# Two more matmuls of 127 columns in each step of the two relation passes of a four-layer graph network

## The reference, cut to what matters

```
h = einsum('ni,rio->rno', x, W)
seg = dst * num_rels + etype
sums = segment_sum(h[etype, src], seg)        # one sum per (node, relation)
cnt = segment_sum(ones, seg)
mean = sums / maximum(cnt, 1)
out = mean.reshape(N, num_rels, do).sum(1) + x @ W_root + b
```

## Time and profile before

| | us |
|---|---|
| median of 3 runs (lowest, highest) | 3812.71 (3811.78, 3816.45) |
| the profiled execution | 3823.57 |
| its span, first to last instruction | 3821.7 |
| mean granted TensorE clock over the span | 0.743 |
| first relation pass, from its first to its last addition on DVE | about 1077 to 2322 |
| dense stage between the passes | about 2322 to 2514 |
| second relation pass | about 2514 to 3759 |

### The profile page before, as it was taken

The page is one execution under the profiler, slowest core; times in us unless marked ns, Lnnn a source line. Parts: engine busy times, 40 slices in busy tenths (PEclk is TensorE's granted clock), DMA queues, the critical chain, the costliest instruction groups (busy, mean ns, idle before and its releaser), DMA issues.

```text
span 3821.7 us, 59833 instructions
## 1 busy us (share of the span) xinstructions
PE 2532.7 (66%) x21427; PEld 1819.2 (48%) x21427; DVE 2517.1 (66%) x6311; ACT 485.3 (13%) x906; POOL 1959.8 (51%) x2108
## 2 busy tenths in 40 slices
PE   3766689989746565666555558965555655656556
PEld 1222265574435444444444446754444444444446
DVE  5999954464267666666666666666666666666667
ACT  2444441151110000000000003510000000000000
POOL 1887800000256666666666662146666666666661
PEclk9999989989865666566666668966666666666667
DMA  1000000000111111111111111111111111111111
GB/s 51 1 1 1 1 6 1 1 2 1 39 52 44 45 44 45 44 45 44 45 45 45 45 45 49 75 60 44 45 44 45 44 45 44 45 45 45 44 45 32
DMA packets 76098, 137.92 MB, mean 36 GB/s; under 512 B 29902, under 2 KB 44640, under 8 KB 75810
## 3 DMA queue, kind: packets, MB, share of 16 engines
q0 software_dynamic: 53120, 108.90, 10.9%
q1 hardware_dynamic: 18934, 24.46, 1.8%
q10 hardware_dynamic: 3756, 0.73, 0.2%
HBM read 116.35 MB, written 17.62 MB: 35 GB/s over the span
## 4 chain that ended last, share of the span: by engine, by line
PE 45%; DVE 28%; issue 11%; another core or an unknown queue 8%; POOL 3%; DMA 2%; ACT 2%; DVEq 1%; ACTq 1%; SPq 0%; POOLq 0%
PE banks L565 26%; DVE adj L1429 15%; DVE hi_hot L1131 6%; PE banks L497 6%; PE banks L490 3%; DVE lo_hot L1139 3%; PE banks L609 2%; POOL adj L711 2%; PE banks L621 2%; DMA adj<-table,adj 2%; PE banks L654 1%; DVEq L1427 1%; PE banks L472 1%; POOL lo_hot L685 1%
## 5 line engine op out<-in xcount | busy, mean ns | idle before, releaser
L565 PE MATMUL banks<-adj 128*128 128x129 f16 x13280 | 1486.3, 291 | 1026.5 <-DVE adj L1429 739.7
L711 POOL DMA_INDIRECT adj<-table,adj x1660 | 1573.3, 948 | 946.8 <-issue 402.1
L565 PEld LDWEIGHTS banks<-adj 128*128 128x128 f16 x13280 | 1199.5, 132 | 1317.9 <-issue 1161.6
L1429 DVE TENSOR_TENSOR adj<-adj,banks 128x516 f32 x1660 | 1143.0, 689 | 844.5 <-PE banks L565 480.7
L1413 DVE TENSOR_SCALAR adj<-adj 128x512 f16<-128x512 f16 x1660 | 697.1, 420 | 0.0
L685 POOL TENSOR_SCALAR lo_hot<-minus_iota,zT 128x128 f16<-128x128 f16 x392 | 332.4, 865 | 140.4 <-PE banks L445 77.1
L445 PE MATMUL banks<-hi_hot,lo_hot 128*128 128x400 f16 x977 | 267.0, 365 | 128.0 <-DVE hi_hot L1131 73.5
L1131 DVE TENSOR_SCALAR hi_hot<-iota,zT 128x400 f16<-128x400 f16 x977 | 266.0, 338 | 21.5 <-PE banks L445 21.4
L692 POOL MEMSET adj<- 128x1548 f16 x1 | 1.4, 1388 | 470.4 <-PE banks L497 470.4
L445 PEld LDWEIGHTS banks<-hi_hot,lo_hot 128*128 128x128 f16 x977 | 97.4, 100 | 297.9 <-issue 240.4
L497 PE MATMUL banks<-adj,split 128*128 128x512 f16 (+1 forms) x1190 | 235.7, 356 | 0.0
(11 more groups left out here) (219 smaller groups left out, 1625.6 us busy)
## 6 DMA issues: line engine op xcount, KB each, us to landing
adj<-table,adj POOLq DMA_INDIRECT x1660
table<-adj SPq DMA_DIRECT2D x25, 512.0 KB, 2.6
table<-split SPq DMA_DIRECT2D x6, 256.0 KB, 2.3
out_dram<-xres SPq DMA_DIRECT2D x6, 256.0 KB
adj<-in_L_gnn_W_dram SPq DMA_DIRECT2D x1, 1024.0 KB, 7.4
adj<-in_L_gnn_W_dram SPq DMA_DIRECT2D x2, 512.0 KB, 9.0
adj<-scr_index SPq DMA_DIRECT2D x1, 830.0 KB
scr_index<-adj SPq DMA_DIRECT2D x1, 512.0 KB
```

Source lines behind the costliest of these rows:

```text
L565: m = e.matmul(ps[:, g * CH // 2:g * CH // 2 + b - a], hot[:, s, g * P:g * P + P], gath[:, s, a:b], start=(q == 0), stop=(q == 1), skip_gr ...
L711: e.indirect_dma_start(gath[:, s, 0:2 * D], None, table, bass.IndirectOffsetOnAxis(ap=index[:, which, j:j + 1].bitcast(U32), axis=0)).then ...
L1429: e.tensor_tensor(a, a, ps[:, :].rearrange("p (g d) -> p g d", g=G)[:, :, 0:D + 1], ALU.add).then_inc(accumulated, 1)
```

## The change

In each step, for the first two of the four blocks, one more matmul follows the two that are there. It has the same stationary operand, 127 columns of the gathered rows as the moving one, and writes the 127 columns of the block's 256 that no instruction reads. The last matmul of a step, which raises `scattered`, stays what it was.

```diff
+FILL = 2
...
                         for q, (a, b) in enumerate([(D, 2 * D + 1), (0, D)]):
                             m = e.matmul(ps[:, g * CH // 2:g * CH // 2 + b - a], hot[:, s, g * P:g * P + P],
                                          gath[:, s, a:b], start=(q == 0), stop=(q == 1), skip_group_check=True)
+                        if g < FILL:
+                            e.matmul(ps[:, g * CH // 2 + D + 1:(g + 1) * CH // 2], hot[:, s, g * P:g * P + P],
+                                     gath[:, s, 0:CH // 2 - D - 1], start=True, stop=True, skip_group_check=True)
                     m.then_inc(scattered, 1)
```

## The result

The changed kernel took 3842.18 us (median of 4 runs, 3838.39 to 3848.62), beside 3814.24 us before (4 runs, 3811.78 to 3816.45): a ratio of 1.0075, 95% interval 1.0058 to 1.0093, so **28 us slower**. I had forecast 3713 us. The profiled execution took 3843.84 us with a span of 3842.0.

What follows compares the result with a forecast made beforehand. Bound: relation passes at 1.50 us a step, above POOL's 1.25 us floor, because completions are seen late. Longer waves at 1.44 save 100 us: 3823.6 - 100 = 3723.6, less 10.9 for the median gives 3713 us; range 3540 to 3885.

Steps and rivals of the forecast that it cites:

- The bound of the kernel: Relation passes: 1.50 us a step, filled by no engine; POOL's gather floor is 1.25; completions are seen late.
- If that phase is what decides, a wave carries one to three more steps: Waves in the passes: completions falling inside a POOL gather are seen in time; pace 1.44 us a step, 100 us less.
- I take 0: Waits for a single step, 320 to 446 of them: added matmuls cost between 0 and 94 us, taken as 0.
- cover: Wave's pause: PE finishes about 0.8 us later, still 1 us ahead of the release, so added matmul time is hidden.
- A faster PE clock as such buys next to nothing here: Single-step waits in the passes: 0.41 us less matmul time was read as starting DVE only 0.01 us sooner.
- the 1.36 and 1.37 us: Times read from a step's first matmul to DVE's start, with 0.61 and 1.02 us of matmuls respectively.
- the bound of 0.35 us: Single-step waits: extra completion time, 1.37 - 1.02, above which added matmuls would delay DVE.
- slower: Rival, lone-step waits and wave starts: later completions shift everything, 58 to 80 us more, 3871 to 3893; chance 0.31.
- the clock would be near 0.8: PE in the passes: ten matmuls per step lift the granted clock from 0.65 to an expected 0.8.
- Same: Rival: release hangs on POOL and DMA events alone, pauses swallow the work; 3813 us within 8; chance 0.22.
- Gather beat: Rival: high clock keeps completions in time, passes run at 1.25 to 1.35 us a step, 3398 to 3564; chance 0.12.
- signs listed: In the profile: L565 x16600, waves of six or more, POOL idle below 947 us, passes about 1195, clock near 0.8.

Runs made afterwards that it cites:

- e15: Kernel before with plain SyncE DMAs for POOL's gathers in the first pass (other rows added) and four bare weight loads per step in the second: 3397.55 us, ratio 0.8898.
- e1: Changed kernel with its two added matmuls cut from 127 columns to 8, same place and count: 21.6 us slower than the kernel before (3816.17 us).
- e2: Kernel before plus four constant-operand matmuls of 127 columns at the start of each step (first pass from step 100): 55.6 us slower than before.
- e3: Kernel before plus four constant-operand matmuls of 127 columns per step, placed behind the matmul that raises scattered: 56.0 us slower than before.
- e4: Kernel before with the high parts' four matmuls of each step left out, so the sums lack them: 66 us less than before (3816.17 us).
- e17: Kernel before plus four bare weight loads per step in both passes, slow kind: 3839.23 us beside 3813.61, ratio 1.0065.
- e18: Kernel before plus eight already satisfied PE wait instructions at the start of each first-pass step: 3806.64 us beside 3784.21, ratio 1.0056.

## Why the prediction was wrong, point by point

**The bound of the kernel** was read rightly as far as it went: no engine fills the 1.50 us, POOL could go at 1.25, and the difference is completions seen late. The fast kind confirms the floor to 0.01 us. That the lateness has to do with POOL's gathers was a guess from the timing of one wave, and e15's first pass bears it out.

**"If that phase is what decides, a wave carries one to three more steps"**: this is the step that failed, and with it the sign. The phase itself moved as forecast, and it bought nothing. Before, on the slow kind, the last matmul of 1138 steps ended (by its modelled end) inside a gather and of 322 in POOL's 0.30 us between two; an update was recorded within 0.3 us for 48% of the first and 2% of the second, so the trace seems to bear the rule out. After, 1319 ended inside and only 18 between, but of the 1319 only 14% were updated that soon; in e1, with two short matmuls, 2% of 1278. On the fast kind it makes no difference where they end: nearly all are prompt. The cost goes by the count each time, whether the added work lies ahead of the completion (e2), behind it (e3) or is a fraction as long (e1). The waves became shorter in steps. The commonest wave of several steps has 5 before, 4 after and in e1, three or four in e2 and e3, and 8 in e4. That is 32 to 48 matmuls, or 64 to 96 matmuls and loads, and it isn't the matmuls alone that end it: bare loads (e17) and satisfied waits (e18's first pass) make waves of 4 with the eight matmuls as they were, and e18's second pass, without the waits, has waves of 5. I had three completions of one wave to rest a rule on, and a rule that needs them to be right to 0.2 us.

**"I take 0" for a lone step, and all edits priced by time on PE.** I priced an added matmul by its length and found cover for all of it. The cover was real: 3320 matmuls of 0.056 us or more are over 180 us, and 28 came through. But on the slow kind each further instruction, matmul or weight load, has a price that no cover takes. The burst spacings, measured apart from the times, give 4.2 ns; with four per step that is 16.8 ns x 1660 = 28 us, the whole result in size, though the recorded bursts hold only a third of it. No row of before shows it, since every step there has the same sixteen; the lower bound of 0 had no measurement under it.

**"A faster PE clock as such buys next to nothing here"** stands, but not for the reason given. The earlier trace rows pair each step's matmuls with the addition of another step. PE may be up to three steps ahead of DVE, and the n-th addition belongs to the n-th step (1660 of each are recorded):

```profile
2599.88 1.77 PE L565 MATMUL banks<-adj 128*128 128x129 f16 x16
...
2607.08 0.69 DVE L1429 TENSOR_TENSOR adj<-adj,banks 128x516 f32 x1
```

The addition at 2605.09 is that of a step begun at 2599.88; the step begun at 2603.73 was added at 2607.08, 3.35 us later, and the one begun at 2612.69 at 2617.37, 4.68 us later. So the 1.36 and 1.37 us measure no step, and with them fall the bound of 0.35 us that "slower" was to be decided by and the argument for 0 at a lone step. In prompt completions (fast kind) the clock is worth 0.41 us a step, 1.20 against 0.79. It buys nothing because the time goes to the late completions on the one kind and to POOL's beat on the other. That the clock would be near 0.8 was right (0.777). The rule of the Trainium skill, "TensorE: Matmul & The Clock Gate", section "A second HAM failure mode: psum-queue depth-cycling", would charge the swing of the clock; with the swing all but gone (0.90 in the passes of the changed kernel on the fast kind, 0.88 overall in e2) nothing came back, so no run here bears it out for this loop.

**The rivals.** "Slower" had the sign, a price of 58 to 80 us where 28 came, and the wrong mechanism: e3 has its four matmuls behind the completion, and pays as much. "Same" is what the fast kind does, though not because pauses swallow the work: there are none. "Gather beat" describes the kernel before itself on that kind, with the low clock that I thought it couldn't have. The range, 3540 to 3885, held the time, 3842. Of the signs listed, L565's count (13280 + 3320) and the clock came as forecast, POOL's idle time rose where it should have fallen, and the wave was the first thing to say that the theory was wrong.

**Left open.** Why a job is of the one kind or the other. By what path POOL's gathers hold up PE's updates, whether it is their issue or their transfers that do it, whether DVE's work beside POOL's has a part in it, and why a wave ends where it does. Whether the 4 ns is spent fetching an instruction, issuing it or retiring it: instruction packets grow with the count in every run (180, 206, 228; 128 in e4), so they can't be told apart; the line of the burst spacings speaks for retiring, but the waits scatter about it. That each step's share stands once in the length of its wave is argued from 16.8 ns = 4 x 4.2, not shown. No version here that fetches the right rows beats both kernels; the plain DMAs would, by 14% on the fast kind, but not with rows picked by an index, and a gather that covers two steps at once wasn't tried.

## What to carry to other kernels

Where a loop is bound by the round trip of small completions, count its instructions, not only their time: on the slow kind each PE instruction, even a wait that is already satisfied, cost 3 to 5 ns though hundreds of microseconds of engine time beside it were free; on the fast kind none cost anything. Matmuls added to hold the clock up can only pay where PE's length is on the path; measure first whether a step at the high clock is seen to end any sooner, and pair each completion with its reader by counting, not by what stands next to it in the timeline. And take before's time anew in each job: the same program differed by 400 us between jobs, and the same change by 28.

## What was unexpected of the hardware

- The same kernel takes 3413 us or 3784 to 3818 us by the job, with nearly all of the difference in the two passes beside POOL's gathers (1042 against 1247 us), and the busy times of DVE and POOL there equal to within 1%.
- On the slow kind the next recorded update of the semaphore comes a median of 1.2 us after a step's last matmul ends, and up to 3.5 us for nineteen steps in twenty, in bursts; the 16 updates of a gather are recorded as about 5 events (8138 / 1660). With plain DMAs from SyncE's queue both are prompt and complete on the same kind.
- The spacing of those bursts is 0.026 us plus 4.2 ns per matmul and per weight load of the step, the same for added matmuls of 8 and of 127 columns.
- A granted clock of 0.90 in place of 0.65 moved passes of 1042 us on the fast kind by nothing.
